# A mixture-of-experts block on one core: the table of pairs one and two tiles later, splits at other tiles

## The reference

```python
# layer 0, cond: 4 experts, two chosen per sample from its sums over tokens; experts 1 and 2 mask a part of the tokens
gate_logits = gate_in @ gate_w + gate_b            # gate_in: means of x over three stretches of tokens
gate_logits = gate_logits * (1.0 + scale) + shift  # from the condition
gate_scores = softmax(gate_logits); topk_w, topk_i = top_k(gate_scores, 2)
topk_w = topk_w / (topk_w.sum(-1) + 1e-8)
for e in range(4):
    h = gelu(c @ ew1[e] + eb1[e]); y = h @ ew2[e] + eb2[e]
    out = out + w_be[:, e] * mask[e] * y
out = out + gelu(c @ sw1 + sb1) @ sw2 + sb2
# layer 0, ffn: 8 experts, all of them, weighted per token
h = silu(x @ w_gate[e]) * (x @ w_up[e]); out += (h @ w_down[e]) * cw[:, e]
# layer 1, cond: 2 shared experts and 8 routed ones (top 2); layer 1, ffn: two low-rank products with a gelu between
```

## Time and profile before

| what | value |
|---|---|
| median of three runs | 901.16 us |
| profiled execution, its own time | 900.65 us |
| its span, first to last instruction | 898.9 us |
| granted TensorE clock, mean | 0.997 |
| TensorE matmul busy | 875.0 us (97%) |
| VectorE, ScalarE, GpSimd busy | 683.0, 576.9, 408.7 us |
| chain of waits | PE 77%, DVE 8%, issue 4%, ACT 3%, DMA 3%, SyncE's queue 2% |

### The profile page before, as it was taken

One profiled execution on the slowest core, in us unless ns is written; L12 is line 12 of the kernel. 1 busy time (PEld: TensorE's weight loads), 2 busy tenths in 40 slices (PEclk: granted clock), 3 DMA queues, 4 the chain that ended last, 5 costly groups with the idle time before them and its releaser, 6 DMA issues.

```text
span 898.9 us, 12685 instructions
## 1 busy us (share of the span) xinstructions
PE 875.0 (97%) x3878; PEld 694.6 (77%) x3878; DVE 683.0 (76%) x1097; ACT 576.9 (64%) x1032; POOL 408.7 (45%) x378
## 2 busy tenths in 40 slices
PE   8899999999999999999999999999999998999996
PEld 5778788878888888888888888888888785777773
DVE  7667777878789786686686686686666876998887
ACT  7788788765555455555555555555555677989896
POOL 7447865035256352252253253253222226755465
PEclk9999999999999999999999999999999999999999
DMA  9588882023023112012012012011010069182640
GB/s 311 195 251 273 297 285 100 1 85 132 13 82 109 36 47 82 1 47 82 1 48 82 1 48 82 1 47 48 7 42 1 0 107 175 39 179 52 159 106 35
DMA packets 35828, 82.96 MB, mean 92 GB/s; under 512 B 4400, under 2 KB 14256, under 8 KB 33840
## 3 DMA queue, kind: packets, MB, share of 16 engines
q1 hardware_dynamic: 35760, 82.15, 30.8%
HBM read 71.13 MB, written 6.83 MB: 87 GB/s over the span
## 4 chain that ended last, share of the span: by engine, by line
PE 77%; DVE 8%; issue 4%; ACT 3%; DMA 3%; SPq 2%; POOL 2%; POOLq 0%; DVEq 0%; ACTq 0%
PE ps L863 17%; PE ps L882 16%; PE ps L868 16%; PE ps L917 8%; PE ps L919 8%; PE ps L912 8%; DMA CWB<-scratch 2%; DVE HL L1462 2%; PE ps L899 1%; PE ps L897 1%; ACT HH L1005 1%; DVE HH L1459 1%; POOL HL L1542 1%; DVE Hf L1449 1%; SPq L722 1%
## 5 line engine op out<-in xcount | busy, mean ns | idle before, releaser
L999 ACT ACTIVATE Sg<-ps 128x512 f32<-128x512 f32 x288 | 171.8, 598 | 246.2 <-PE ps L882 245.8
L1442 DVE TENSOR_TENSOR Hf<-ps,Sg 128x512 f32<-128x512 f32 x288 | 198.0, 688 | 149.1 <-ACT Sg L999 93.2
L1542 POOL TENSOR_TENSOR HL<-Hf,HH 128x512 fp32r<-128x512 f32 x136 | 182.3, 1347 | 172.4 <-ACT HH L1005 154.6
L1005 ACT ACTIVATE HH<-Hf 128x512 fp32r<-128x512 f32 x346 | 216.2, 625 | 24.9 <-DVE Hf L1442 12.9
L1462 DVE TENSOR_TENSOR HL<-Hf,HH 128x512 fp32r<-128x512 f32 x242 | 214.7, 887 | 4.2 <-ACT HH L1005 3.2
L863 PE MATMUL ps<-XHL,WBH 128*128 128x512 f32 x512 | 203.7, 398 | 1.2 <-DVE Hf L1442 1.2
L882 PE MATMUL ps<-XHL,WBH 128*128 128x512 f32 x512 | 202.1, 395 | 0.0
L868 PE MATMUL ps<-XHL,WBL 128*128 128x512 f32 x512 | 202.0, 395 | 0.0
L1557 POOL TENSOR_TENSOR XT<-XT,TMP 128x512 f32<-128x512 f32 x64 | 84.2, 1316 | 251.5 <-DVE TMP L1338 251.5
L863 PEld LDWEIGHTS ps<-XHL,WBH 128*128 128x128 f32 x512 | 96.1, 188 | 25.1 <-DVE Hf L1442 2.3
L882 PEld LDWEIGHTS ps<-XHL,WBH 128*128 128x128 f32 x512 | 96.0, 188 | 23.1
(11 more groups left out here) (254 smaller groups left out, 1347.3 us busy)
## 6 DMA issues: line engine op xcount, KB each, us to landing
CWB<-scratch SPq DMA_DIRECT2D x68, 256.0 KB, 7.9
CWB<-scratch SPq DMA_DIRECT2D x15, 1024.0 KB, 4.7
GWD<-expert_down SPq DMA_DIRECT2D x21, 576.5 KB, 4.6
GWU<-expert_up SPq DMA_DIRECT2D x21, 514.0 KB, 5.1
ST<-in_wb_dram SPq DMA_DIRECT2D x8, 768.0 KB, 6.3
GX<-XT SPq DMA_DIRECT2D x68, 64.0 KB, 2.8
XT<-in_x_dram SPq DMA_DIRECT2D x8, 256.0 KB, 5.3
expert_up<-GWU SPq DMA_DIRECT2D x4, 512.0 KB, 3.8
```

The lines of the kernel that those rows point to most:

```text
L999: e.activation(Sg[:, it.n % NG, :], zb[z % NZ][:, :], ACT.Silu).then_inc(s_act, 1)
L1005: e.activation(HH[:, it.n % NH, 0:it.cols], hidden_place(it), ACT.Copy).then_inc(s_hi_act, 1)
L1442: e.tensor_tensor(Hf[:, it.n % NS, :], zb[z % NZ][:, :], Sg[:, it.n % NG, :], ALU.mult).then_inc(s_prod, 1)
L1542: e.tensor_tensor(HL[:, it.n % NH, :], Hf[:, it.n % NS, :], HH[:, it.n % NH, :].bitcast(F32), ALU.subtract).then_inc(s_lo_pool, 1)
```

## The change

The numbers are slots. The counting matmuls go from slot 12 to 13, the key from 13 to 14, the step behind it (`g_past`) from 14 to 15, the table's sums from 16 to 18, the index from 17 to 19, the gates' weights from 16 to 20 (so behind the index and not ahead of it), their product with the table from 18 to 21, its sums from 20 to 22, their copy from 21 to 23, and SyncE's first load from 18 to 20. The exponential stays at 12. The splits of blocks 6 and 7 go from tiles 1 and 3 of groups 2 and 6 to the third tiles of groups 2, 3, 7 and 8; those of expert 0's weights from tile 4 of group 9 and tiles 1 and 2 of group 10 to the third tiles of groups 12, 13 and 15.

```diff
--- before.py
+++ after.py
@@ -293,20 +293,20 @@
         spilled = {}
         for t, (i, h) in split_wa.items():
             spilled.setdefault(t + 2, []).append((i, h))
-        first_load = 18
+        first_load = 20
         split_x = {0: (2, 3), 7: (4,), 17: (5,)}
 
-        g_in, g_best, g_top, g_exp, g_sort, g_key, g_past, g_table = 9, 10, 11, 12, 12, 13, 14, 16
-        g_gate, g_index, g_both, g_gates, g_weight = 16, 17, 18, 20, 21
-        split_end = {pos["G", 2, 0, 0].k: (6, 0), pos["G", 2, 0, 2].k: (6, 1), pos["G", 6, 0, 0].k: (7, 0),
-                     pos["G", 6, 0, 2].k: (7, 1)}
+        g_in, g_best, g_top, g_exp, g_sort, g_key, g_past, g_table = 9, 10, 11, 12, 13, 14, 15, 18
+        g_index, g_gate, g_both, g_gates, g_weight = 19, 20, 21, 22, 23
+        split_end = {pos["G", g, 0, 2].k: s for g, s in ((2, (6, 0)), (3, (6, 1)), (7, (7, 0)), (8, (7, 1)))}
 
         split_g = {pos["G", g - 1, 0, 0].k if g else pos["G", 0, 0, 0].k - 1: g for g in range(NGRP)}
         first_b = [pos["B", 0, ex, 0].k for ex in range(8)]
         text = first_b[2]
         fill_b = {pos["G", 8, 0, 0].k: 0, first_b[0] + LAG + 10: 1}
         fill_b |= {first_b[ex - 1] + 2: ex for ex in range(2, 8)}
-        split_wb = {t + 7 + k: (ex, k) for t, ex in fill_b.items() for k in range(3)}
+        split_wb = {t + 7 + k: (ex, k) for t, ex in fill_b.items() if ex for k in range(3)}
+        split_wb |= {pos["G", g, 0, 2].k: (0, k) for k, g in enumerate((12, 13, 15))}
         c0 = first_b[1] + LAG + 12
         fill_c = {c0: 0, c0 + 1: 1, c0 + 4: 2, c0 + 6: 3}
         split_wc = {c0 + 2: (0, 0), c0 + 3: (0, 512), c0 + 4: (1, 0), c0 + 5: (1, 512)}
```

## The result

The changed kernel takes 903.41 us, the median of 20 runs (901.83 to 904.77); the kernel before 901.12 us in 20 runs beside it. The ratio is 1.0025, with a 95% interval of 1.0018 to 1.0032: slower by 0.25%, some 2.3 us. The profiled execution took 904.03 us, its span 902.2 us [before: rows 1].

What follows compares the result with a forecast made beforehand. Bound: TensorE, with SyncE's index and token transfers on the path setting the end. Late index +3.9, wait at 62.89 −0.42, expert 0's weights −1.97: +1.5 us, forecast 902.7 us (+0.17%), range 899.0 to 905.3.

Steps and rivals of the forecast that it cites:

- The path: SyncE reads the index, then issues token transfers without pause; a late index delays group 3's tokens and TensorE by 3.9 us.
- The key behind tile 12's low part: VectorE's key chain, 3.52 us, starts at 29.0 and ends at 32.5; TensorE waits 2.7 us at tile 17.
- The index's lateness: VectorE's index chain starts 3.9 us later than 35.74; ends 2.6 (no clock fall) and 4.2.
- The wait at 62.89: TensorE's wait behind VectorE's subtraction L1204 goes when that moves to group 3: 0.42 us back, bounds 0 and 0.42.
- Block 7's subtraction: VectorE's split pair moved to groups 7 and 8, called full; no shown wait hangs on it, counted as nothing.
- Expert 0's weights: GpSimd's low parts, each alone in a full group, remove TensorE's waits at 100.00 and 105.41: 1.97 us, bounds 0 and 1.97.
- The sum: Whole kernel: +3.9 − 0.42 − 1.97 = +1.5 us on a span of 898.9; forecast 902.7 us, +0.17%.
- Hidden transfers (1): Group tokens lie ready early, so a late index costs nothing: −2.4 us, 898.8 us; chance 0.12.
- a GpSimd queue that can't take the splits (4): Splits of expert 0's weights overload GpSimd: 906.8 us, or 904.7 if merely nothing is gained; chance 0.12.
- Rivals 2 and 3: No clock fall at tile 17: 901.4 us, chance 0.17; a second fall at tile 27: 903.1 to 904.2 us, chance 0.14.

Runs made afterwards that it cites:

- the second profile: The changed kernel run again, unaltered, against the kernel before: 902.99 against 900.28 us, ratio 1.003.

## Why the prediction was right, and where it was off

- **The path.** That the index sets when the tokens land, and that these set the time, is shown twice: making only the index late costs 5.3 us, and giving it back one slot in the changed kernel takes away 1.9 of its 2.3 us. What the prediction left out is that the table's own waits would cost some 2 us even with the index in time; in the changed kernel they are hidden behind the tokens.
- **The key behind tile 12's low part.** 32.5 us was forecast for its end, and the low part behind it starts at 32.52; tile 17 was put at 33.15 and starts at 33.25. The wait of tile 15 (0.9) and of 17 (2.7) are 0.72 and 2.43 by the column, 0.87 and 2.60 by distance.
- **The index's lateness** was the mis-sized term: 3.9 us taken, 4.4 in the profile with the fall at tile 17, 3.0 in those without. Both ends, 2.6 and 4.2, were too small. With the fall, tile 18 started at 37.33 in place of 36.7 to 37.2 (the prediction's own terms, 35.6 and up to 1.8, go to 37.4), and its activation came 1.01 us later in place of 0.89. Without it, in the second profile, three terms were short by a little over 0.1 us each: tile 17 started 0.12 later than forecast, tile 18 2.63 behind it in place of 2.5, and the index 2.82 behind that in place of 2.7. In the profiles without the fall at tile 17 the forecast's size is luck: 3.0 us came by the index and 1.7 by a fall behind tile 27, and the sum, 4.4 to 4.6 at tile 34, is near the 3.9 that were to come by the index alone.
- **The wait at 62.89.** 0.42 us were taken back; with the waits near it 0.75 came (splits alone 1.0). At its new place in group 3 the subtraction took 0.79 us, not the 1.40 that the prediction had it hide.
- **Block 7's subtraction** was priced at nothing. That was wrong: in group 8 it took 1.38 us on VectorE, and of the three low parts queued behind it TensorE waited for one at tile 61, in a small group whose tiles follow each other sooner; 0.5 us in every run that has it there. Where it stands in group 7 that step is missing, but 0.2 came before tile 60. The prediction also called the groups it leaves full, which group 6 is not (256 columns). VectorE's timeline:

```profile
93.66 1.38 DVE L1204 TENSOR_TENSOR XHL<-XT,XHL 128x512 fp32r<-128x512 f32 x1
94.96 1.95 DVE L1462 TENSOR_TENSOR HL<-ps,HH 128x512 fp32r<-128x512 f32 x3
```

- **Expert 0's weights.** 1.97 us were forecast; 1.8 to 1.9 came between tiles 61 and 72 in the runs with these splits. Blocks 6 and 7 alone have 0.5 there, so the weights' own share is better read from the whole stage: 2.35 less 0.60, 1.75 us. GpSimd takes the low part and is through with the mask product before VectorE wants it; the token split follows without a wait ahead of it, so the queue there has no idle time left, but nothing behind it waits:

```profile
112.97 1.28 POOL L1495 TENSOR_TENSOR WBL<-ST,WBH 128x512 fp32r<-128x512 f32 x1
114.22 0.61 POOL L1528 TENSOR_TENSOR WM<-GWD,WP 128x256 f32<-128x256 f32 x1
114.80 0.74 POOL L1537 TENSOR_TENSOR GHL<-GX,GHL 128x256 fp32r<-128x256 f32 x1
```

- **The sum.** +1.5 us was forecast against +2.3 in the medians (+3.3 in the profiled execution, 0.8 of it the chance landing). By the table the missing 0.8 us is what arrives at tile 34 (4.5 in place of 3.9) and the subtraction in group 8 (0.5), less 0.3 more gained at tile 37.
- **The rivals.** Hidden transfers (1) and a GpSimd queue that can't take the splits (4) are refuted. Rivals 2 and 3 are not: the clock falls behind the wait at tile 17 or behind that at tile 27, in different executions of the same kernel. I had them as separate cases, one cheaper and one dearer. In the three profiles with the changed table and the index at 19 one fall comes in one place or the other, and the lateness at tile 34 is 4.4 to 4.6 us either way; with only the index late both falls came, as before's own is one of them.

## What to carry to other kernels

Follow a moved step to the end of its consumers before counting the wait in front of it: here two waits of TensorE were removed by setting back a step whose result another queue, serially busy for 20 us, was waiting for. When every engine goes through its program in order, look first for what holds the queue ahead of the step, here two loads of ScalarE's table that could stand elsewhere, rather than for a later slot. And when moving filler work, look at what the other engines run beside it and who needs the bank or buffer a few tiles on, not only at whether its own tile is roomy.

## What was not expected of the hardware

- The granted clock fell in one execution of the changed kernel and not in the other behind the same wait: at tile 17 after 2.43 us in the first and not after 2.44 in the second, at tile 27 not after 2.19 in the first and after 1.86 in the second. The shortest wait behind which it fell in these runs is 1.45 us (ahead of L769, exponential at 15). With the index at 18 it stayed down twice as long behind the same 2.44 us. The Trainium skill (TensorE: Matmul & The Clock Gate, "What's actually happening") says that the watching is free-running and isn't reset by the kernel's start; that the place of the fall differs between these two profiles agrees with it.
- The same transfer of 577 KB (GWD for group 11) took 7.2 us to land in one execution of the changed kernel and 4.5 in the other.
- VectorE's subtraction L1204, on operands of one size, took three different times, and in all profiles here they go with what GpSimd was doing. Started 0.2 us behind GpSimd's mask product (L1528) it took 1.37 to 1.40 us (60.84 in the earlier trace rows, and group 8 in the changed kernel). Started 0.3 us ahead of it, for block 7 in the kernel before (80.33), it took 0.91, and the mask product 1.50 in place of 1.05. Started in the middle of GpSimd's additions (L1552), in group 3 of the changed kernel and in group 7 where block 7 stands there, it took 0.79 to 0.80, and the four additions 2.17 in place of 1.72. So the two slow each other, and by how much depends on which starts first; no run changes this alone.
